# Attention written out batch by batch, with the score maxima turned in two halves and SyncE's issue order changed

## The reference, cut to what matters

```python
q = (x @ wq).reshape(b, s, NH, HD)      # x = layernorm(h), NH = 32 heads of HD = 32
k = (x @ wk).reshape(b, s, NKV, HD)     # NKV = 8, each shared by NREP = 4 heads
v = (x @ wv).reshape(b, s, NKV, HD)
scores = jnp.einsum('bihd,bjhd->bhij', q, jnp.repeat(k, NREP, axis=2)) * SCALE
scores = jnp.where(causal, scores, jnp.finfo(scores.dtype).min)
attn = jax.nn.softmax(scores, axis=-1)
out = jnp.einsum('bhij,bjhd->bihd', attn, jnp.repeat(v, NREP, axis=2))
```

## Time and profile before

| | us |
|---|---|
| median of 3 runs (lowest, highest) | 3302.35 (3300.98, 3305.52) |
| the profiled execution | 3308.47 |
| its span, first to last instruction | 3306.7 |

### The profile page before, as it was taken

One profiled execution on the slowest core, in us unless ns is written; L12 is line 12 of the kernel. 1 busy time (PEld: TensorE's weight loads), 2 busy tenths in 40 slices (PEclk: granted clock), 3 DMA queues, 4 the chain that ended last, 5 costly groups with the idle time before them and its releaser, 6 DMA issues. The chain is left out here.

```text
span 3306.7 us, 81949 instructions
## 1 busy us (share of the span) xinstructions
PE 2939.5 (89%) x28864; PEld 2155.8 (65%) x29056; DVE 2001.8 (61%) x4714; ACT 1113.0 (34%) x2452; POOL 1027.9 (31%) x1402
## 2 busy tenths in 40 slices
PE   1847799998899899899999986699999999999999
PEld 1637688888888888888888873245445445445444
DVE  7975577777677767777777764443444444444443
ACT  4331345554555455454555554200101001001000
POOL 3730244444444444444444453010110111011010
PEclk9978899999999999999999996599999999999999
DMA  4643222322222222222222223112212212212211
GB/s 149 172 124 102 56 78 58 83 57 79 58 78 58 77 76 59 79 56 79 57 80 57 73 59 123 51 58 76 68 65 76 72 61 76 75 58 76 76 57 47
DMA packets 235387, 249.64 MB, mean 75 GB/s; under 512 B 169752, under 2 KB 196504, under 8 KB 234784
## 3 DMA queue, kind: packets, MB, share of 16 engines
q1 hardware_dynamic: 234768, 234.69, 24.0%
q10 hardware_dynamic: 240, 10.09, 0.9%
HBM read 114.26 MB, written 80.61 MB: 59 GB/s over the span
## 5 line engine op out<-in xcount | busy, mean ns | idle before, releaser
L734 POOL TENSOR_SCALAR_AFFINE_SELECT p<-p 128x256 f32<-128x256 f32 (+1 forms) x768 | 334.3, 437 | 878.7 <-ACT p L762 856.8
L844 DVE TENSOR_REDUCE mx<-psS 77x2 f32<-77x410 f32 (+1 forms) x768 | 449.6, 613 | 228.4 <-PE psS L949 142.8
L967 PE MATMUL psJ<-xth,qh 128*128 128x205 f16 x2048 | 531.4, 259 | 19.6 <-DVE qsl L852 17.0
L969 PE MATMUL psJ<-xth,ql 128*128 128x205 f16 x2048 | 527.2, 257 | 0.0
L968 PE MATMUL psJ<-xtl,qh 128*128 128x205 f16 x2048 | 525.5, 257 | 0.0
L762 ACT ACTIVATE p<-psT,escale 128x410 f32<-128x410 f32 (+1 forms) x768 | 410.9, 571 | 278.8 <-PE psT L908 208.6
L740 POOL TENSOR_TENSOR pl<-p,ph 128x410 f16<-128x410 f32 (+1 forms) x512 | 446.2, 892 | 106.9 <-ACT ph L769 99.3
L1300 POOL TENSOR_TENSOR hb<-h,bias_sb 128x1024 f32<-128x1024 f32 x52 | 122.2, 2349 | 1044.7 <-DVE h L1342 1044.7
L1342 DVE SCALAR_TENSOR_TENSOR h<-ps5O,osc,h_in 128x512 f32<-128x512 f32 x104 | 78.1, 751 | 428.3 <-PE ps5O L1389 428.3
L769 ACT CAST ph<-p 128x410 f16<-128x410 f32 (+1 forms) x768 | 334.2, 500 | 9.0 <-POOL p L734 9.0
L1387 PE MATMUL ps5O<-woh,ath 128*128 128x512 f16 x832 | 316.6, 381 | 1.4 <-DVE atl L1327 1.4
(11 more groups left out here) (243 smaller groups left out, 6092.7 us busy)
## 6 DMA issues: line engine op xcount, KB each, us to landing
a_in<-acat SPq DMA_DIRECT2D x52, 512.0 KB, 4.8
h_in<-hcat SPq DMA_DIRECT2D x52, 512.0 KB, 4.2
qst<-qsh SPq DMA_DIRECT2D x512, 51.2 KB, 2.1
out<-y SPq DMA_DIRECT2D x51, 512.0 KB, 3.0
hcat<-ob SPq DMA_DIRECT2D x64, 256.0 KB, 3.7
xin<-hcat SPq DMA_DIRECT2D x32, 512.0 KB
acat<-ao SPq DMA_DIRECT2D x32, 512.0 KB
qst<-qsl SPq DMA_DIRECT2D x256, 51.2 KB, 2.1
```

What stands on the lines that cost most here:

```text
L734: pool.affine_select(out=v, in_=v, compare_op=ALU.is_ge, fill=0.0, base=0, pattern=[[0, v.shape[1]], [1, w]], channel_multiplier=-1).then_ ...
L844: dve.tensor_reduce(dst, v, AX.X, ALU.max).then_inc(s_read, 1)
L967: pe.matmul(ps[:, 0:S], wh[:, k, c], xth[:, par, k, :], start=k == 0, stop=False)
L969: m = pe.matmul(ps[:, 0:S], wl[:, k, c], xth[:, par, k, :], start=False, stop=k == KC - 1)
```

## The change

The loop is written out: every engine's step is built for each b from -3 to 32, waits compare with constants, and the semaphore `passed` with its increments is gone. The maxima take one group in each of the eight slots. The unit m becomes two: `("m", 0)` turns the maxima of heads 0 to 15 in slot 4 of the step in which they are found; `("m", 1)` turns those of heads 16 to 31 in slot 0 of the next step, as that slot's third unit. Each half is sent by `shift_rows` with a semaphore of its own; `scores` waits for the first in slot 0 and for the second in slot 4. SP's order in a step becomes: Q half 1, V, K half 1, the late maxima, load, store, Q half 0, the early maxima, K half 0. DVE waits before it overwrites the maxima of heads 16 and up until the late unit has read them.

```diff
-        mh, ml = sb("mh", [NH, S], F16), sb("ml", [NH, S], F16)
+        mh, ml = sb("mh", [NH // 2, 2, S], F16), sb("ml", [NH // 2, 2, S], F16)
...
-        MAXES = [[0], [1], [2], [3], [4, 5], [6, 7], [], []]
+        MAXES = [[j] for j in range(NKV)]
...
+                if s == 0 and has["att"]:
+                    row.append(("m", 1))
                 if s >= 4 and has["ln"]:
                     row.append(("x", s - 4))
-                if s == NKV - 2 and has["max"]:
+                if s == 4 and has["max"]:
                     row.append(("m", 0))
...
         def steps(eng, step):
-            for b in range(-3, 2):
-                step(b, b % 2, parts(b))
-            with eng.Fori(1, 14) as i:
-                step(i * 2, 0, FULL)
-                step(i * 2 + 1, 1, FULL)
-            for b in range(28, B + 1):
+            for b in range(-3, B + 1):
                 step(b, b % 2, parts(b))
...
             if kind == "m":
-                wait(eng, m_in, 32 * (b + 1))
+                wait(eng, m_in[n], 32 * (b + 1 - n))
...
                     wait(sp, pj_lo, before(b - 1, nxt) + at(units(prev), "q", NKV - 1) + 1)
-                    restack(K_PARTS, kst[nxt], slice(1, 2), k_in[1])
                     restack(Q_PARTS, qst[nxt], HALVES[1], q_in[1])
-                if has["load"]:
-
-                    wait(sp, pj_filled, base)
-                    pass_on(sp, passed)
-                    load(b + 4, par)
-                if has["max"]:
 
                     wait(sp, av_done, 8 * b)
-                    pass_on(sp, passed)
                     sp.dma_start(vh[nxt][:], vsh[:]).then_inc(v_in, 16)
                     sp.dma_start(vl[nxt][:], vsl[:]).then_inc(v_in, 16)
-                if early and b == -1:
+                    restack(K_PARTS, kst[nxt], slice(1, 2), k_in[1])
+                if has["att"]:
+
+                    wait(sp, pj_lo, base + at(rows, "m", 1) + 1)
+                    shift_rows(1, par)
+                if has["load"]:
+
+                    wait(sp, pj_filled, base)
+                    load(b + 4, par)
+                if b == -1:
...
                     restack(Q_PARTS, qst[par], HALVES[0], q_in[0])
+                if has["max"]:
+
+                    wait(sp, pj_lo, base + at(rows, "m", 0) + 1)
+                    shift_rows(0, nxt)
+                if has["qkv"]:
+
                     wait(sp, pj_lo, base + at(rows, "k", 0) + 1)
                     restack(K_PARTS, kst[par], slice(0, 1), k_in[0])
-                if has["max"]:
-
-                    wait(sp, pj_lo, base + at(rows, "m") + 1)
-                    sp.dma_start(qst[nxt][STACK:STACK + 1, :, :], mh[:]).then_inc(m_in, 16)
-                    sp.dma_start(qst[nxt][STACK + 1:STACK + 2, :, :], ml[:]).then_inc(m_in, 16)
+
+            def shift_rows(half, to):
+                heads = slice(half * (NH // 2), (half + 1) * (NH // 2))
+                sp.dma_start(qst[to][STACK:STACK + 1, heads, :], mh[:, half, :]).then_inc(m_in[half], 16)
+                sp.dma_start(qst[to][STACK + 1:STACK + 2, heads, :], ml[:, half, :]).then_inc(m_in[half], 16)
...
+                    if j == NKV // 2 and k == 0 and late_read:
+
+                        dve.wait_ge(pj_filled, base + late_read)
...
-                if g == 0 and k == 0:
+                if g % 4 == 0 and k == 0:
 
-                    pe.wait_ge(m_in, 32 * (b + 1))
+                    pe.wait_ge(m_in[g // 4], 32 * (b + 1))
...
-                    pe.wait_ge(s_read, 24 * (b + 2))
-                    pe.transpose(ps[0:NH, 0:P], mx[:, 0, :], ident[:])
-                    m = pe.transpose(ps[0:NH, P:S], mx[0:TXT, 1, :], ident[0:TXT, 0:TXT])
+                    heads = slice(n * (NH // 2), (n + 1) * (NH // 2))
+                    pe.wait_ge(s_read, 24 * (b + 1) + 12 * (1 - n))
+                    pe.transpose(ps[0:NH // 2, 0:P], mx[:, 0, heads], ident[:])
+                    m = pe.transpose(ps[0:NH // 2, P:S], mx[0:TXT, 1, heads], ident[0:TXT, 0:TXT])
```

More of the change, by code:

```diff
@@ L521, in attention @@
         cleared, lo_pool = sem("cleared"), sem("lo_pool")
-        passed = sem("passed3")
         pool_c, dve_c, dve_ln, const_ok = sem("pool_c3"), sem("dve_c3"), sem("dve_ln"), sem("const_ok")
@@ L531, in attention @@
         k_in = [sem(f"k_in{c}") for c in range(2)]
-        m_in, v_in = sem("m_in"), sem("v_in")
+        m_in, v_in = [sem("m_in0"), sem("m_in1")], sem("v_in")
         a_out = [sem("a_out0"), sem("a_out1")]
         SLOTS = range(NKV)
-        MAXES = [[0], [1], [2], [3], [4, 5], [6, 7], [], []]
+        MAXES = [[j] for j in range(NKV)]
         EXTRA = {0: ("k", 0), 1: ("k", 1), 2: ("v", 0), 3: ("v", 1)}
@@ L560, in count @@
             return sum(map(len, units(parts(b))))
-        FULL = parts(2)
-        PER = count(0)
         BEFORE = {b: sum(count(c) for c in range(-3, b)) for b in range(-3, B + 2)}
         def before(b, par):
-            return BEFORE[b] if isinstance(b, int) else BEFORE[2] - 2 * PER + b * PER
+            return BEFORE[b]
         def odd(b, par):
-            return (BEFORE[b] if isinstance(b, int) else BEFORE[2 + par]) % 2
+            return BEFORE[b] % 2
         def at(rows, kind, n=0):
@@ L608, in unit_views @@
             if kind == "m":
-                return ps[0:NH, 0:S], mh[:], ml[:]
+                return ps[0:NH // 2, 0:S], mh[:, n, :], ml[:, n, :]
             t, half = divmod(n, 2)
@@ L642, in step @@
                 rows = units(has)
-                early = isinstance(b, int)
                 nxt = 1 - par
@@ L647, in step @@
                     wait(sp, st_filled, 24 * b)
-                    pass_on(sp, passed)
-                    prev = parts(b - 1) if early else FULL
+                    prev = parts(b - 1)
                     wait(sp, pj_lo, before(b - 1, nxt) + at(units(prev), "q", NKV - 1) + 1)
+                    restack(Q_PARTS, qst[nxt], HALVES[1], q_in[1])
+                    wait(sp, av_done, 8 * b)
+                    sp.dma_start(vh[nxt][:], vsh[:]).then_inc(v_in, 16)
+                    sp.dma_start(vl[nxt][:], vsl[:]).then_inc(v_in, 16)
                     restack(K_PARTS, kst[nxt], slice(1, 2), k_in[1])
-                    restack(Q_PARTS, qst[nxt], HALVES[1], q_in[1])
+                if has["att"]:
+                    wait(sp, pj_lo, base + at(rows, "m", 1) + 1)
+                    shift_rows(1, par)
                 if has["load"]:
                     wait(sp, pj_filled, base)
-                    pass_on(sp, passed)
                     load(b + 4, par)
-                if has["max"]:
[L660 to L663, removed]
-                if early and b == -1:
+                if b == -1:
                     for dst, src, arrived in ahead:
@@ L729, in step @@
                         pool.wait_ge(exp_done, 24 * b + 3 * g + k + 1)
-                        pass_on(pool, passed)
                         v = view(p32, g % 2, k)
@@ L818, in layer_norm @@
                     for h in range(2):
-                        chain(dve.bn_stats(stats[0:T[g], g, h, :], x[0:T[g], g, 512 * h:512 * h + 512]), passed)
+                        chain(dve.bn_stats(stats[0:T[g], g, h, :], x[0:T[g], g, 512 * h:512 * h + 512]))
                     chain(dve.bn_aggr(mv[0:T[g], g, :], stats[0:T[g], g]))
@@ L830, in layer_norm, with take_maxes @@
                     dve.sem_inc(dve_ln, 2)
-            def take_maxes(b, j, base, ks):
+            def take_maxes(b, j, base, ks, late_read):
                 for k in ks:
@@ L858, in step @@
                 late = None
+                late_read = at(rows, "m", 1) + 1 if has["att"] else 0
                 for g in SLOTS:
@@ L861, in step @@
                     for j in groups[:1]:
-                        take_maxes(b, j, base, (0, 1))
+                        take_maxes(b, j, base, (0, 1), late_read)
                     if late:
@@ L866, in step @@
                     for j in groups[:1]:
-                        take_maxes(b, j, base, (2,))
+                        take_maxes(b, j, base, (2,), late_read)
                     if has["att"]:
```

## The result

The changed kernel takes 3371.06 us (median of 4 runs, 3360.41 to 3375.93) against 3303.93: it is slower, ratio 1.0195 with a 95% interval of 1.0164 to 1.0226. The direction and the place were forecast.

What follows compares the result with a forecast made beforehand. Bound: the attention step, PE busy 1466 of 1597.6 us. Terms: 49.4 + 0.5 + 5.5 + 2.2 = 57.6 us a step, 1728 for 30, +130; first step +3; +133 in all gives 3435 us, range 3390 to 3480.

Steps and rivals of the forecast that it cites:

- the maxima's term: Slots 4 to 7: moving two groups to slots 6 and 7 costs 0, upper end 1.8 us a step.
- the stall's: Slot 2, PE behind ACT's late ksh copy: 5.5 us idle plus 2.2 us of reduced clock a step.
- SP's order: K half 1 lands at +20.5, making ACT's slot 1 copy 6.5 us late; PE idles 5.5 us in slot 2.
- Base and halves: Full attention step without stall: 49.4 us base plus 0.5 us for the additional unit of the maxima's halves.
- The sum: Attention step: 49.4 + 0.5 + 5.5 + 2.2 = 57.6 us; 30 steps 1728 us, first step +3, together +133.
- Rival 3: Cheap stall in slot 2: 3.3 us with 1.7 of clock, 3354 us, or 5.5 with clock kept, 3370; chance 0.16.
- Loop written out: Attention loop: back edges, their reduced clock and register waits go; 30 steps take 1482 us, 116 less.
- base step 1858.5: Step outside the old loop, 49.4 us, with all PE work and V in time, lacking only a load.
- rival 4: Second thing late: slower K half 1 blocks, 3540 us, or K half 0 1.2 us late each step, 3471; chance 0.12.
- rival 5: Fetching straight-line code starves an engine: 1.4 us a step on top, 3477 us; chance 0.02.

Runs made afterwards that it cites:

- e1: Changed kernel with SP's order K half 1, V, Q half 1 in place of Q half 1, V, K half 1; 3177.1 us, ratio 0.9621 to the kernel before.
- e2: Changed kernel, its SP order kept, with two places for ksh and ksl that alternate by batch; 3176.7 us, ratio 0.9622 to the kernel before.
- e3: As e1, but the maxima again take two groups in slots 4 and 5 and none in 6 and 7; 3210.7 us, ratio 0.9720.
- e7: Kernel before, written out, with SP's order K half 1, V, Q half 1, load; neither spread maxima nor halves; 3200.6 us, ratio 0.9672.
- e4: Kernel before with only its loop written out; order, maxima and turns as before; 3274.4 us, ratio 0.9906.
- e8: Changed kernel with K half 1 moved on SP behind the late maxima, the load and the store; 3512.0 us, ratio 1.0625 to the kernel before.
- e9: e1 put back into the loop of 13 passes over two steps, with the increments of passed; 3283.1 us, ratio 0.9909 to the kernel before.

## Why the prediction was wrong in size and right in kind

Two steps of the prediction failed: the maxima's term, put at 0, and the stall's, 7.7 us a step, which was too large.

- **SP's order: right.** Each link came as forecast, and e1 and e2 show both ends of the chain: the late transfer and the copy's place.
- **Size of that term: too large, by 35 us.** Idle and clock were 5.5 + 2.2 = 7.7 us a step and are 6.53 (changed kernel against e1; in steps 2 to 29 6.72). The idle, 5.24 in these, was nearly right: the K block took 8.06 us from its first to behind its last issue, not 8.6. The clock costs 1.99 in slot 2, not 2.2. And slot 3 takes 0.41 less than in e1, for which the prediction has no term: e1's wait for a remainder there (L966, 7.5 us in all, some 0.25 a step) is all but gone (0.4), presumably because the matmuls before it run slower. Slot 0 accounts for the remaining 0.1.
- **Maxima one group per slot: wrong, by 31 us.** "PE's sum stays ... I take 0" is the step that failed: it is -1.05 us a step. Slots 4 to 7 take 20.40 us in the changed kernel and in e1, 21.56 in e3. The prediction bounded the term above only, and counted PE's instructions where the slots' fill sets the waits. The trace of the kernel before held a hint, waits for a remainder in its light slot 6:

```profile
PE psJ L982 <- DVE qsl L852: 26.0, 29, 0.9
```

- **Base and halves: right.** A full step was put at 49.4 + 0.5 = 49.9; e3, which has just these parts and no stall, takes 49.78 in steps 2 to 29, and the halves are 0.44 of it. With 0.1 for the first step's own waits 50.0 were forecast for the mean of 30, and e3 has 50.19.
- **The sum.** 57.7 forecast a step ((1728 + 3) / 30), 55.67 measured: 1.05 + 1.17 (7.7 - 6.53) - 0.19 = 2.03, the whole difference; over 30 steps 61 us of the missing 66. The rest is the stretch's start, 5.5 us earlier than before, which the forecast didn't count.
- **A number met by luck.** Rival 3 has 3370 us for a stall of 5.5 with the clock kept. The time is near it, but the clock was not kept: it was 0.50 behind the idle. The agreement is chance.
- **Loop written out: right in the end, for the sum.** In e7, with steps of 49.34 us, PE waits without a semaphore for 0.2 us in all, so straight-line code shows no cost. But the 116 us credited to it need V in time, which the new order supplies: alone it is worth 31 us (e4). The base step 1858.5 has no load in front of V in SP's order. In e4 steps 1 to 27 have that load and PE waits for V in each; steps 28 and 29 have none, and there is no such wait.
- **K half 0 late (rival 4): hardly.** PE's wait at L946 in slot 0 is 1.7 us in four steps behind the first (8.4 - 6.7), where these keys landed 0.65 to 1.11 us into the step; the rival had 1.2 us in every step. **Fetching (rival 5):** no sign.

## What to carry to other kernels

When the issue order of a queue is changed, list for every transfer not only who reads what it brings but who overwrites what it takes away: here nobody needed the keys before slot 4, and the copy that reused their source needed them gone in slot 1. A wait that disappears may have been covering another one (the jump and V), so price an edit in the order that the other edits leave. When work is spread over slots, look at the waits of the lightest slot, not only at the sum of the busiest engine.

## What the runs showed of the chip that was not expected

- The reduced clock behind a stall cost nearly the same for three lengths of it: 2.08, 1.99 and 2.09 us in slot 2 for idles of 3.90, 5.24 and 9.45 us. Behind one idle of 4.64 us the granted clock was 0.50 for 3.4 us and 0.81 in the next 3.4.
- A jump back over a two-batch body cost PE 3.7 us of idle (44.4 / 12). The loop with all that it brings, other waits and reduced clock among them, cost 102 us of the stretch (e9 against e1).
- SP issued twelve DMAs of keys in 8.06 us in the changed kernel and in 8.76 in e8, where they stand behind a load and a store (means of steps 2 to 29).
